# Recommendation network on one core: products of features in two halves with a step of layer 1 between, and another order of the first block

## What is computed

```
e = emb_tables[jnp.arange(F)[None, :], x]            # (1024, 32, 64)
gram = jnp.einsum('bid,bjd->bij', e, e)
cross = gram[:, iu, ju]                              # 496 pairs
h = jnp.concatenate([e.reshape(B, F * D), cross], axis=1)
h = jax.nn.relu(h @ W1 + b1)                         # 2544 -> 1024
h = jax.nn.relu(h @ W2 + b2)                         # 1024 -> 512
return jax.nn.sigmoid(h @ W3 + b3)                   # 512 -> 1000
```

## Time and profile before

| | us |
|---|---|
| median of 3 runs | 429.7 (426.57 to 430.92) |
| the profiled execution, whole | 430.89 |
| its span, first to last instruction | 429.0 |
| TensorE busy | 386.4 |
| VectorE busy | 289.4 |
| ScalarE busy | 250.0 |
| GpSimd busy | 238.8 |
| mean granted clock of TensorE | 0.967 of full |

### The profile page before, as it was taken

The page is one execution under the profiler, slowest core; times in us unless marked ns, Lnnn a source line. Parts: engine busy times, 40 slices in busy tenths (PEclk is TensorE's granted clock), DMA queues, the critical chain, the costliest instruction groups (busy, mean ns, idle before and its releaser), DMA issues.

```text
span 429.0 us, 7544 instructions
## 1 busy us (share of the span) xinstructions
PE 386.4 (90%) x2906; PEld 327.1 (76%) x2906; DVE 289.4 (67%) x503; ACT 250.0 (58%) x394; POOL 238.8 (56%) x240
## 2 busy tenths in 40 slices
PE   0586976995999997999999999899999999999996
PEld 0575865784789886788889987788889987788894
DVE  4679795774657955676668855867568767654652
ACT  3545464643566776545666777637576587544642
POOL 6888884087577777487767774367668720000000
PEclk9889796999899998999999999999999999999999
DMA  7845556289565977299785877498775865695512
GB/s 244 273 130 163 157 157 202 81 273 284 161 196 149 249 215 217 67 281 303 222 228 164 256 214 223 134 253 291 221 221 172 246 178 187 215 271 189 156 44 95
DMA packets 34866, 85.65 MB, mean 200 GB/s; under 512 B 6544, under 2 KB 13648, under 8 KB 34320
## 3 DMA queue, kind: packets, MB, share of 16 engines
q1 hardware_dynamic: 28048, 78.22, 58.0%
q0 software_dynamic: 6784, 6.96, 7.7%
HBM read 76.86 MB, written 8.29 MB: 198 GB/s over the span
## 4 chain that ended last, share of the span: by engine, by line
PE 56%; POOL 21%; issue 7%; DVE 5%; ACT 5%; DMA 4%; SPq 1%; DVEq 0%; POOLq 0%; ACTq 0%
POOL emb L423 19%; PE h1p L673 12%; PE h1p L675 11%; PE h1p L674 11%; PE misc L666 3%; PE misc L668 3%; PE misc L667 3%; PE misc L675 3%; PE misc L673 3%; PE misc L674 3%; ACT wsplit L441 2%; DVE dg L582 2%; PE misc L742 2%; POOL gap L414 2%; PE misc L720 2%
## 5 line engine op out<-in xcount | busy, mean ns | idle before, releaser
L423 POOL DMA_INDIRECT emb<-tables_dram,idx x212 | 229.6, 1083 | 106.4 <-issue 54.9
L558 DVE TENSOR_TENSOR wsplit<-wraw,wsplit 128x512 fp32r<-128x512 f32 (+1 forms) x224 | 143.7, 686 | 74.2 <-ACT wsplit L441 73.2
L441 ACT CAST wsplit<-wraw 128x1024 fp32r<-128x1024 f32 (+1 forms) x112 | 117.4, 1048 | 55.5 <-PE h1p L675 39.7
L673 PE MATMUL h1p<-wsplit,xhi 128*128 128x512 f32 x256 | 107.4, 420 | 0.0
L674 PE MATMUL h1p<-wsplit,xlo 128*128 128x512 f32 x256 | 104.4, 408 | 0.0
L675 PE MATMUL h1p<-wsplit,xhi 128*128 128x512 f32 x256 | 104.1, 407 | 0.0
L675 PEld LDWEIGHTS h1p<-wsplit,xhi 128*128 128x128 f32 x256 | 50.2, 196 | 12.4
L673 PEld LDWEIGHTS h1p<-wsplit,xhi 128*128 128x128 f32 x256 | 50.4, 197 | 11.0
L674 PEld LDWEIGHTS h1p<-wsplit,xlo 128*128 128x128 f32 x256 | 50.2, 196 | 10.7
L453 ACT COPY z<-misc 64x256 f32<-64x256 f32 (+1 forms) x108 | 42.0, 389 | 10.4 <-DVE xlo L564 9.5
L631 DVE TENSOR_SCALAR hot<-xb,vals 128x512 fp32r<-128x512 int32 x88 | 38.5, 508 | 3.0 <-DMA xb<-xt_dram 3.0
(11 more groups left out here) (50 smaller groups left out, 483.9 us busy)
## 6 DMA issues: line engine op xcount, KB each, us to landing
wraw<-w_dram SPq DMA_DIRECT2D x96, 512.0 KB, 4.6
wraw<-w_dram SPq DMA_DIRECT2D x16, 500.0 KB, 4.3
wraw<-tables_dram SPq DMA_DIRECT2D x11, 512.0 KB, 6.1
gram_scratch<-dg SPq DMA_DIRECT2D x4, 1024.0 KB, 5.0
out_dram<-res SPq DMA_DIRECT2D x16, 250.0 KB, 2.1
emb<-tables_dram,idx POOLq DMA_INDIRECT x212, 3.9
xb<-xt_dram SPq DMA_DIRECT2D x11, 256.0 KB, 5.2
gc<-gram_scratch SPq DMA_DIRECT2D x16, 64.0 KB, 4.2
```

What stands on the lines that cost most here:

```text
L423: nc.gpsimd.indirect_dma_start(emb[:, n % 2, k, t, f * D:(f + 1) * D], None, tables, bass.IndirectOffsetOnAxis(ap=idx[:, BT * n + t, 2 * k ...
L441: nc.scalar.copy(whi(u % RING, w), wraw[:, u % RAWS, 0:w]).then_inc(s_whi, 1)
L558: last = nc.vector.tensor_tensor(wlo(u % RING)[:, part], wraw[:, u % RAWS, part], whi(u % RING)[:, part].bitcast(fp32), ALU.subtract)
L673: nc.tensor.matmul(dst, hi, whi(slot)[:, cols], start=start, stop=False, skip_group_check=True)
```

## The change

In `products` the item `gram` becomes two: `gram` (groups 0 and 1) and `rest` (groups 2 and 3), with a step `emb` between them (`emb` 5 in block 0, `emb` 8 in the others). ScalarE's and VectorE's copies are split in the same way, and the write to DRAM moves from `gram` to `rest`. The next items keep their kinds: in block 0 the step taken for the middle is one that came before `gram` until now; in blocks 1 to 3 it is one that came after it, and `move` now follows `emb` 11 in place of `emb` 10.

In `first_block` the look-up is followed by the step of the iteration before (`emb` k-1) ahead of the transposition, and the eight comparisons go in three lots (3, 3 and 2) around these.

```
     def first_block():
-        yield ("ones", 0, 0)
+        yield ("ones", 0, 0, 0, VC)
         for k in range(5):
+            more = k < 4
             yield ("look", 0, 11 + k)
+            if more:
+                yield ("ones", 0, k + 1, 0, 3)
+            if k > 0:
+                yield from emb(0, k - 1)
+            if more:
+                yield ("ones", 0, k + 1, 3, 6)
             yield ("tr", 0, k)
-            if k < 4:
-                yield ("ones", 0, k + 1)
-            yield from emb(0, 11 + k, k)
+            if more:
+                yield ("ones", 0, k + 1, 6, VC)
+            yield from emb(0, 11 + k)
         yield ("tr", 0, 5)
-        yield from emb(0, 5)
+        yield from emb(0, 4)
...
     def products(n):
         more = n + 1 < BLOCKS
         yield ("gram", n)
-        yield from emb(n, *((6, 7) if n == 0 else (8,)))
+        yield from emb(n, 5 if n == 0 else 8)
+        yield ("rest", n)
+        yield from emb(n, 6 if n == 0 else 9)
         if more:
-            yield ("ones", n + 1, 0)
-        yield from emb(n, *((8, 9) if n == 0 else (9, 10)))
+            yield ("ones", n + 1, 0, 0, VC)
+        yield from emb(n, *((7, 8) if n == 0 else (10, 11)))
         yield ("move", n)
         yield from l3(n - 1, 2)
-        yield from emb(n, *((10,) if n == 0 else (11, 12)))
+        yield from emb(n, *((9, 10) if n == 0 else (12,)))
         yield ("pairs", n)
...
+    HALVES = {"gram": range(GROUPS // 2), "rest": range(GROUPS // 2, GROUPS)}
...
-                if kind == "gram":
+                if kind == "rest":
                     if n > 0:
                         sp.wait_ge(s_gc, 128 * n)
                     sp.wait_ge(s_dga, GROUPS * (n + 1))
...
-                if kind == "gram":
+                if kind in HALVES:
                     if n > 0:
                         act.wait_ge(s_gdw, 16 * n)
-                    gram_copies(n)
+                    gram_copies(n, HALVES[kind])
...
-                if kind == "gram":
-                    gram(n)
+                if kind in HALVES:
+                    gram(n, HALVES[kind])
```

More of the change, by code:

```diff
@@ L73, in later_block @@
         yield ("th", n - 1, 3)
-        yield ("ones", n, 1)
+        yield ("ones", n, 1, 0, VC)
         yield from l2(n - 1, 0)
@@ L462, in looked_up_hi, with gram_copies @@
                 nc.scalar.copy(xlo[0:D, k, :], read[D:P, 0, :]).then_inc(s_lookhi, 1)
-            def gram_copies(n):
-                for g in range(GROUPS):
+            def gram_copies(n, groups):
+                for g in groups:
                     act.wait_ge(s_gram, GROUPS * n + g + 1)
@@ L623, in h2_split, with compare @@
                 split(h2f, h2hi, h2lo, j, (s_h2f, 4 * n + 2 * j + 2), s_h2hi, 2 * n + j + 1, s_h2lo)
-            def compare(i):
+            def compare(i, first, last):
                 dve.wait_ge(s_xb[i % 2], 16 * (i // 2 + 1))
@@ L629, in compare @@
                     dve.wait_ge(s_used, used_after(*LOOKED[i - 1]))
-                for c in range(VC):
+                for c in range(first, last):
                     nc.vector.tensor_scalar(hot[:, :, c, :], xb[:, i % 2, :, :],
@@ L634, in _ @@
             dve.wait_ge(s_vals, 1)
-            compare(0)
+            compare(0, 0, VC)
             for u in range(AHEAD):
@@ L643, in _ @@
                 if kind == "ones" and (n, k[0]) > (0, 0):
-                    compare(LOOK["look", n, LOOKED_UP[n][k[0]]])
+                    compare(LOOK["look", n, LOOKED_UP[n][k[0]]], *k[1:])
                 if kind == "tr":
@@ L724, in look_up, with gram @@
                 return last
-            def gram(n):
+            def gram(n, groups):
                 before = SLOTS[:slots_before(("gram", n))]
[L728 to L734, removed]
+                if 0 in groups:
+                    pe.wait_ge(s_ztr, sum(slot in TR for slot in before))
+                    pe.wait_ge(s_zlook, sum(slot in LOOK for slot in before))
+                    if n > 0:
+                        pe.wait_ge(s_h1lo, sum(slot in TH for slot in before))
+                        pe.wait_ge(s_biased, 2 * outs_before(("gram", n)))
+                for g in groups:
                     if g >= 2:
```

## The result

The changed kernel takes 426.65 us in the median of 11 runs (422.30 to 429.09), the kernel before beside it 430.31 us (426.57 to 433.82): a ratio of 0.9896 with a 95% interval of 0.9852 to 0.9941, so about 4.5 us less (2.5 to 6.4). Ratios, here and in the experiments, are taken over the runs in the faster of a program's two states alone, while the medians hold all runs, so the two can differ a little. The forecast was 7.2 us less. The sign was right, and 426.65 lies inside the range, close to its upper end of 427.0, but the main term was put too high: 7.2 us would be a ratio of 0.983, outside the interval.

A forecast was written before the change was run, and what follows sets the result against it. TensorE's work plus its idle time bounds the kernel. Gains of 4.4 us in block 0 and 3.3 in blocks 1 to 3, less 0.5, make 7.2: 429.7 to 422.5 us, 8-in-10 range 418.5 to 427.0.

The forecast's parts named there:

- 3.3 less 0.5 in all: Blocks 1 to 3: halves gain 1.1 us each, 3.3 together; 0.5 us lost to waits at the first `pair` step.
- the cover of the way through DRAM: Blocks 1 to 3, behind `rest`: one step of 2.81 us less, against 2.5 us spare in block 1, 1.9 in block 3.
- `move` would go out sooner by the missing split: Block 0: one weight split fewer ahead, 1.85 us, and copies 0.8 us earlier put `move` at 92.9 instead of 95.51.
- the wait of the last transposition of block 1: At 167.45 before: TensorE still waits about as long, and the 4.4 us gain arrives there whole.
- the first block's order: Block 0: reordering steps, transpositions and comparisons gains 0 up to 68.39, bounded by 1 us either way.
- the 4.4 us of block 0: `pair` 0 ends at 107.1, so GpSimd is released at 107.3 instead of 111.70; bounds 2.2 to 5.3 us.
- GpSimd's own work doesn't bind: Block 1's early gathers: GpSimd finishes pair of tiles 1 at 106.4, before its release at 107.3.
- just in time at 73.6: Block 0, `tr` 5: its last gather, issued about 69.2, lands at 72.7 after 3.5 us, ahead of 73.6.
- the full clock: Block 0, `pair` 0: after waits of 1.7 and 1.8 us TensorE runs at full rate, taking 2.8 us.
- the prediction's sum was 5.0 us: Half clock at `pair` 0 of block 0: release about 2.2 us later, total gain 5.0 us in place of 7.2.
- Rival 4: Block 0: landings at 68.39 or `tr` 5 1 to 2 us late, clock falls at `pair` 0; 3.5 us gain, 426.2; chance 0.08.
- The slower rival: Blocks 1 to 3: the way through DRAM becomes the bound at `pair` 0; 4.8 us slower, 434.5; chance 0.05.

The follow-up runs named there:

- first group: Four of the twelve follow-up kernels, run on one chip beside the kernel before, which takes 467.65 us there.
- before again: The kernel before, run once more with no edit, against itself: ratio 1.0028 (0.9992 to 1.0064).
- third group: Four more follow-up kernels, run on another chip beside the kernel before, which takes 464.19 us there.
- early release: The changed kernel with the gathers of block 1 let go earlier, against the kernel before: ratio 0.9874 (0.9831 to 0.9918), median 424.20 us.
- second group: Four more follow-up kernels, run on another chip beside the kernel before, which takes 431.19 us there.

## Why the prediction was right, and where it was too high

**Right.** The two halves in 2.10 us each. The stalls taken: 1.3 us a block in blocks 1 and 2 (185.76 - 183.18 over two) and 0.8 in the last; I had 3.3 less 0.5 in all, and it is 3.4. That the cover of the way through DRAM would be used up in blocks 1 to 3 and just hold: 0.36 us spare in block 1 and a release at the last moment in block 3. That `move` would go out sooner by the missing split. That the wait of the last transposition of block 1 wouldn't shrink but move: 2.35 and 2.29 us (4.94 with block 0 alone). That the first block's order is worth nothing measurable.

**Too high: the 4.4 us of block 0.** The step that failed is the sentence that GpSimd's own work doesn't bind. Measured alone, the change in block 0 gives 1.7 us (0.2 to 3.2). With the halves in block 0 alone GpSimd was done with its 16 gathers at 109.40, where the prediction had 106.4. The 3.0 us are made up of two things:

1. The dot products ended 1.1 us later than forecast (the first gather at 85.42 in place of 84.3), since `tr` 5 waited. It was forecast as just in time at 73.6, on the assumption of 3.5 us from the issue of its last gather at 69.2 to its landing. In three of the six profiles with the new order and halves in block 0 it waits, 1.35, 1.39 and 2.91 us, and the dot products start at 77.5, 78.0 and 79.1 (the last, on the first group's chip, with another wait in between). With block 0 alone that gather was issued at 70.78, 1.6 us later than assumed, and landed 3.8 us behind that. In the kernel before this transposition came at 76.42, almost 3 us later, and there an issue at 71.30 cost nothing (the profile of before again). In the first profile of the changed kernel `tr` 5 came at 71.95 without a wait, because the fifth transposition had come 1.3 us early and its gather was issued at 69.41; I take that for most of the reason why this run was the fastest.
2. GpSimd's 16 gathers from the end of the dot products on. I took the 22.1 us of the old trace over (107.58 - 85.50), and that was the shortest of all: in the five profiles with whole dot products in block 0 and the gathers released as before it is 22.1 to 23.1 us (22.9 in before again). In the six with halves there it is 23.1 to 24.0. The means are 22.7 and 23.6, so about 0.9 us belongs to the change and the rest is scatter. In the first profile GpSimd was done at 106.25, 0.44 us ahead of its release; with block 0 alone at 109.40, 1.6 us behind the end of the pair step that was to release it (104.98 and 2.81 us of work), and what the read-back had gained there was lost.

The new list puts two weight splits right behind the comparisons with no pause, where the old had one, and the longest of the 16 gathers is then 2.80 us in all six profiles, and 2.38 or 2.39 in all five with whole dot products. In the kernel before, GpSimd's gather and VectorE's split:

```profile
93.49 2.39 POOL L423 DMA_INDIRECT emb<-tables_dram,idx  x1 [0.30 <-issue]
```

```profile
93.77 1.28 DVE L555 TENSOR_TENSOR wsplit<-wraw,wsplit 128x512 fp32r<-128x512 f32 x2
```

The split ends at 95.05 and the gather at 95.88, 0.83 us behind. In the changed kernel the two splits end at 90.58 + 1.28 = 91.86 and the gather at 89.88 + 2.80 = 92.68, 0.82 us behind; the gather of 3.38 us in before again ended 0.83 us behind three splits in a row. So the second split costs this gather 0.4 us. The other half of the 0.9 us is a few tenths in each of several gathers, and which instruction costs them isn't shown. The Trainium skill (SBUF — State Buffer, Who interferes with whom) says that a VectorE instruction with two inputs in SBUF contends with a GpSimd instruction that reads SBUF. The splits have two such inputs and the gather reads its indices there, and these three endings agree with it. The rule as it stands, though, isn't all of it: the gather at 88.01 in the kernel before began beneath a split too (87.54 to 88.83) and took 1.04 us.

**The clock.** I took the full clock behind two waits of 1.7 us. In the first profile they were 2.22 and 0.48 us and the stretch behind was granted 0.50; in the run with block 0 alone they were 2.55 and 0.50 us and the first pair step ran at 0.23 us a product, full rate. So nearly the same waits went both ways, but not equally often: of the six profiles with halves in block 0 and the gathers released as before, five begin the first pair step at half rate. Half rate was what the forecast should have counted on; it is the case for which the prediction's sum was 5.0 us. With block 0 alone the full clock gained nothing, since GpSimd's own pace bound. In the third group's profile of the changed kernel the half rate did decide: the first pair step started at 104.31, as forecast, ran at 0.50, and GpSimd, done at 108.73, waited 1.26 us for its end. That is the lower bound I had given this term (2.2 us), less the landing of `tr` 5.

**Sum.** 1.7 and 3.4 make 5.1 us, inside the measured 2.5 to 6.4. The 1.7 is a measured time; the 3.4 is read from two profiles, against a forecast of 2.8, and made up for some of what block 0 fell short. Rival 4, a late landing at `tr` 5 and the clock falling at `pair` 0, is the nearest to what took the rest: the first half of it shows in three of the profiles, both halves in two of these. What it left out is GpSimd's own pace, and it blamed the first block's order, where the last gather's issue scatters in either order (69.2 to 72.2 us in the old, 69.3 to 70.8 in the new). The slower rival did not come.

**What stays open.** Whether the first block's order costs up to 0.7% or gives it. How the early release compares with the changed kernel: 0.9874 against 0.9896 was measured in different groups of runs, and the intervals overlap. What the halves of blocks 1 to 3 give in time on their own: the one run of them lost 0.6%, on a chip with pauses, against the profiles elsewhere.

## What to carry to other kernels

When a step is pulled forward to fill a hole, ask what it was covering. Here it had hidden a wait of 1.4 us and more for a late gather, and in the later blocks 2.5 us of a way through DRAM. A forecast that moves one release earlier has to time the engine that is released over again as well, its own work included, with what it will now lie beside: GpSimd's 22.1 us became 23.1 to 24.0, in part because two of VectorE's weight splits moved together, and in part because 22.1 was itself a lucky reading. And one profile is one run: where the runs of a kernel spread over 1.6%, two profiles can differ by twice the gain.

## What the runs showed of the hardware that I had not expected

**Chips differ.** The same program takes 430 us where the result and the second group were measured, and 464 to 468 us on the chips of the first and third group. What is added is pauses of TensorE at a few places of the program. Some have no semaphore behind them; others are waits for ScalarE or VectorE, which stood still themselves (5.99 us for `h1lo` in the stretch below). In the third group's profile of the changed kernel, the worst stretch:

```profile
128.30:146.20 17.90, 7.33 (x33) 7.00 (x33) 4.02 (x7) 5.05 (x9) 9.64 (x11) 0.64 0.21 51
```

33 products in 17.9 us, with the DMA engines 0.21 busy; in both profiles of the kernel before, TensorE is busy through all of the 17.9 us from 128.3, with 123 and 124 products. I have no measurement of the cause.

**A GpSimd chain can be exact.** From its release to the issue of the 39th gather behind it, GpSimd took 53.15, 53.14, 53.13 and 53.14 us in four profiles, on kernels with differing orders, while that last gather took 2.55 to 3.8 us from its issue to the transposition that waited for it. All four are from undisturbed chips; in the seven profiles of the slower chips with this release the same stretch took 56.8 to 63.5 us.

**A gather can wait for VectorE.** Most gathers took 0.94 us on GpSimd. One that was under way as one, two or three weight splits followed without a pause took 2.39, 2.80 and 3.38 us, and ended 0.82 or 0.83 us behind the last split each time.
